# Attention: where the second norm's root stands on GpSimd and its normalisation on VectorE

## Chip, cores and metric

The kernel runs on one core of a Trainium2 chip. The metric is the device time of one execution in microseconds (us), as the median of several runs.

## What is computed

A "macaron" block over 32 sequences of 256 tokens of width 128, in float32: `x += 0.5*ffn(ln(x))`, then `x += attention(ln(x))`, then `x += 0.5*ffn(ln(x))`. The feed-forward is a mixture of 8 experts: each token goes to the expert of its largest affinity, and only the tokens of the highest ranks within the sequence are kept. Attention is causal, with 16 heads of width 8. Cut to what matters here:

```python
def _layernorm(x, axis=-1, eps=1e-05):
    m = jnp.mean(x, axis=axis, keepdims=True)
    v = jnp.var(x, axis=axis, keepdims=True)
    return (x - m) / jnp.sqrt(v + eps)

# attention, on ln(x)
q, k, v = (split_heads(q), split_heads(k), split_heads(v))
att = jnp.einsum('bhqd,bhkd->bhqk', q, k) * scale
att = jnp.where(causal[None, None] == 0, big_neg, att)
att = jax.nn.softmax(att, axis=-1)
x = jnp.einsum('bhqk,bhkd->bhqd', att, v)
# routing of the feed-forward that follows, on ln of the new x
num = jnp.einsum('bsd,ed->bse', inputs, waff)
x_norm = jnp.linalg.norm(inputs, axis=-1, keepdims=True)
aff = num / (x_norm * w_norm[None, None, :] + 1e-09)
ranks = jnp.argsort(jnp.argsort(-aff, axis=1), axis=1)
```

## The kernel before

The program has five stages, each behind a barrier: token statistics, routing, experts, attention with the routing of the second feed-forward, experts again. The change touches attention alone (some 275 to 860 us of the profile).

Attention is a software pipeline written out by hand. `run` (L1207) calls `turn(b, k, has)` on every engine for b from -4 to 35. A turn has NP = 12 steps, `u` = 0 to 11, and works on several sequences at once; `has(o)` says whether sequence b + o exists. Every engine executes its own list in program order, and semaphores join the lists. What a turn does, by sequence:

- b + 4 and b + 3: gather `xa` (GpSimd, steps 2 and 3, L1283), first norm, Q and K in bfloat16 parts (ScalarE L1371, VectorE L1697, L1711), V.
- b + 2 and b + 1: scores by query for the row maxima. TensorE writes one tile `pp` in each step (`scores_by_query`, L1430 to L1437; `QUERY_TILES`, L1121, names which), VectorE reduces it to maxima (L1678). There are two `pp` buffers: a tile waits until the maxima of the tile two before it are done. In steps 0 to 4 these are tiles 7 to 11 of sequence b + 1, in steps 5 to 11 tiles 0 to 6 of b + 2. The maxima go through GpSimd (L1328 to L1334, step 5), TensorE (L1552), ScalarE (L1398) and a transfer on SP's queue (L1231) into `qs` (TensorE's next step 0 waits for that, L1444).
- b: scores by key into `pm` (L1448, L1452), exponential on ScalarE (L1360), causal mask on GpSimd (L1276: `affine_select` on the tile `pt`, one in each step), products with V on TensorE (`times_v`, L1469; tile group 0 in step 6, group 1 in step 9, groups 2 and 3 in steps 0 and 3 of the next turn).
- b - 1: output projection, sum `x2` (VectorE L1727, step 9), `bn_stats` (step 10), mean and variance and then `vare2` (L1592, step 11; it increments `var2`).
- b - 2: the second norm. GpSimd in step 0 raises `vare2` to the powers -0.5 and 0.5 (L1288, increments `rstd2`) and multiplies out `size` (L1290). VectorE in step 2 normalises `x2` to `xn2`, two instructions (helper line L1651, called at L1692). TensorE transposes them in step 3 (L1484, behind `times_v`), ScalarE copies the result out (L1366), TensorE multiplies with the router's weights in step 7 (L1493), VectorE forms affinities in step 8 (L1611).
- b - 3 and b - 4: ranking. VectorE L1623, L1626, L1637, L1641 and `beats` L1687 in steps 0 and 1; GpSimd scatters rows in steps 7 and 9 (L1322).

On VectorE a step runs `route_a`, `place_a`, the maxima of the step's tile, `route_b`, `place_b`, and then the further work. On GpSimd a step begins with the mask. On TensorE a step runs the `pp` tile, the `pm` tile, `times_v` where due, and then `small(u)`, where L1484 is.

Of the kernel before, what the change touches and what calls it, by code (L numbers as in the profile page):

```python
# [14 lines left out]
ALU = mybir.AluOpType  # L15
# [4 lines left out]
D = 128  # L20
# [3 lines left out]
TPB = S // P  # L24
# [14 lines left out]
NQ = 4  # L39
# [10 lines left out]
class Mem:  # L50
# [17 lines left out]
    def sb(self, name, shape, dt=F32):  # L68
        return self.ctx.enter_context(self.nc.sbuf_tensor(name, shape, dt))
# [1031 lines left out]
def attention(nc, m, io, c, x_dram):  # L1101
# [9 lines left out]
    with ctx:  # L1111
# [13 lines left out]
        xa, xr, x2 = two("xa", [P, TPB, D + 2]), two("xr", [P, TPB, D]), [sb(f"x2{k}", [P, TPB, XW]) for k in range(NQ)]  # L1125
        bn, vare = two("bn", [P, TPB, 6]), two("vare", [P, TPB])
        bn2, vare2 = two("bn2", [P, TPB, 6]), two("vare2", [P, TPB, 2])
        xn, xt = two("xn", [P, TPB, D]), two("xt", [P, S])
        xn2, x2t = two("xn2", [P, TPB, D]), two("x2t", [P, S])
# [7 lines left out]
        powers, mhalf = sb("powers", [P, TPB, 2]), sb("mhalf", [P, TPB])  # L1137
# [55 lines left out]
        def wait(eng, s, n, most=None):  # L1193

            n = n if most is None else min(n, most)
            if n > 0:
                eng.wait_ge(s, n)
# [62 lines left out]
        def _(pool):  # L1260
            g = nc.gpsimd
# [6 lines left out]

            def turn(b, k, has):
                for u in range(NP):  # L1270
                    if has(0):

                        wait(pool, exped, b * NP + (u + 1))
                        n = 4 if u % 3 == 2 else 2
                        tile = pt[u % RING][:, :].rearrange("p (h q) -> p h q", h=n)[:, :, 0:P]
                        g.affine_select(out=tile, in_=tile, compare_op=ALU.is_ge, fill=0.0, base=0,  # L1276
                                        pattern=[[0, n], [1, P]], channel_multiplier=-1).then_inc(masked, 1)
                    if u in (2, 3) and has(4):
                        n, j = b + 4, u - 2
# [4 lines left out]
                                                bass.IndirectOffsetOnAxis(ap=c.place[:, n * TPB + j:n * TPB + j + 1], axis=0)).then_inc(xa_in[k % 2], 16)  # L1284
                    if u == 0 and has(-2):
                        n, q = b - 2, k % 2
                        wait(pool, var2, n + 1)
                        g.tensor_tensor(x2[(k - 2) % NQ][:, :, D + 1:D + 3], vare2[q][:, :, :], powers[:, :, :], ALU.pow).then_inc(rstd2, 1)  # L1288
                        wait(pool, rstd2, n + 1)
                        g.tensor_tensor(size[q][:, :], x2[(k - 2) % NQ][:, :, D + 1], x2[(k - 2) % NQ][:, :, D + 2], ALU.mult).then_inc(size_done, 1)  # L1290
                    if u == 1 and has(-2):
# [11 lines left out]
                    if u == 3 and has(-3):  # L1303
                        n, q = b - 3, (k - 3) % 2
# [7 lines left out]
                    if u == 10 and has(-3):  # L1312
                        q = (k - 3) % 2
                        wait(pool, spot_got, b - 2)
                        g.tensor_copy(to[(k - 3) % NQ][:, :], spot_of[q][:, :]).then_inc(to_done, 1)
                    if u in (7, 9) and has(-4):
                        n, j = b - 4, (u - 7) // 2
# [6 lines left out]
                    if u == 5 and has(1):  # L1324
                        n, q = b + 1, (k + 1) % 2
# [9 lines left out]
                    if u == 8 and has(4):  # L1335
                        wait(pool, var1, b + 5)
                        g.tensor_tensor(xa[k % 2][:, :, D + 1], vare[k % 2][:, :], mhalf[:, :], ALU.pow).then_inc(rstd1, 1)

            run(turn)

        @blk.scalar
# [237 lines left out]
        def _(dve):  # L1579
# [39 lines left out]
            def place_a(n, q, u):  # L1619

                if u == 0:
                    wait(dve, aff_done, n + 1)
                    v.tensor_reduce(amax[n % NQ][:, :], aff[:, :, :], axis=AX.X, op=ALU.max).then_inc(amax_done, 1)  # L1623
                if u == 1:
                    wait(dve, weighed, TPB * n + TPB)
                    v.tensor_reduce(wmax[:, :], weight[:, :, :], axis=AX.X, op=ALU.max).then_inc(wmax_done, 1)  # L1626
                if u == 8:
                    wait(dve, turned_out, n + 1)
                    v.tensor_tensor(spot[:, :, :], mr[:, S:S + TPB * E].rearrange("p (j e) -> p j e", e=E),
                                    c.hots[q][:, 0:3 * TPB:3, :], ALU.mult).then_inc(own_spot, 1)  # L1630
# [18 lines left out]
            def normalise(out, x, done):  # L1649
                for j in range(TPB):  # L1650
                    v.scalar_tensor_tensor(out[:, j, :], x[:, j, 0:D], x[:, j, D:D + 1],  # L1651
                                           x[:, j, D + 1:D + 2].to_broadcast([P, D]), ALU.subtract, ALU.mult).then_inc(done, 1)
# [8 lines left out]
            def turn(b, k, has):  # L1661
                for u in range(NP):
                    if has(-2):
                        route_a(b - 2, k % 2, u)
                    if has(-3):
                        place_a(b - 3, (k - 3) % 2, u)
                    for o, w in QUERY_TILES[u]:
                        if has(o):
                            n, q = b + o, (k + o) % 2
                            wait(dve, pre_done, n * NP + (w + 1))  # L1670
                            if w == 0:
                                wait(dve, mp_done, n - 1)
                            if w < 4:
                                out = mx[q][:, 0, :, 2 * w:2 * w + 2].rearrange("p r g -> p g r")
                                src = pp[w % 2].rearrange("p (g r q) -> p g r q", g=2, r=2)
                            else:
                                out, src = mx[q][:, 1, :, w - 4], pp[w % 2].rearrange("p (r q) -> p r q", r=2)
                            v.tensor_reduce(out, src, axis=AX.X, op=ALU.max).then_inc(maxed, 1)  # L1678
# [4 lines left out]
                    if u in (0, 1) and has(-4):  # L1683
                        n, j = b - 4, u
# [1 line left out]
                        wait(dve, ranked, n * TPB + j)  # L1686
                        v.scalar_tensor_tensor(beats[j][:, :], mr[:, j * S:(j + 1) * S], amax[k][:, j:j + 1], c.tie[:, j, :],  # L1687
                                               ALU.subtract, ALU.is_gt, accum_out=x2[k][:, j, RANK:RANK + 1]).then_inc(ranked, 1)
                    if u == 2 and has(-2):
                        wait(dve, rstd2, b - 1)  # L1690
                        wait(dve, x2t_tr, (b - 3) * TPB)
                        normalise(xn2[k % 2], x2[(k - 2) % NQ], xn2_done)  # L1692
                    if u == 3 and has(3):
                        h = (k + 1) % 2
                        wait(dve, a_done, b + 4)
# [3 lines left out]
                    if u == 5 and has(-1):  # L1699
                        q = (k - 1) % 2  # L1700
# [7 lines left out]
                    if u == 5 and has(3):  # L1708
                        q = (k + 1) % 2
# [12 lines left out]
                    if u == 9 and has(-1):  # L1722
                        q = (k - 1) % 2
# [8 lines left out]
                    if u == 11 and has(-1):  # L1732
                        q = (k - 1) % 2
                        wait(dve, rstd2, b - 2)
                        statistics(b - 1, x2[(k - 1) % NQ], bn2[q], vare2[q], bnd2, mv2, var2, True)

            run(turn)
            s = Steps(dve, settled)
            dve.wait_ge(summed, B)
# [76 lines left out]
```

## Time and profile before

| | us |
|---|---|
| median of 3 runs | 1015.39 |
| range of the runs | 1014.93 to 1016.19 |
| the profiled execution | 1012.83 |
| its span | 1011.1 |
| mean granted clock of TensorE | 0.955 |

Busy over the whole span: TensorE 87% (weight loads 66%), VectorE 74%, ScalarE 59%, GpSimd 68%. Stretches differ: attention keeps TensorE and VectorE above 90%, the stages around it do not. So the shares of the whole span say little for one stage; the rows below are read from attention. Durations are of one execution. An instruction shown as x2 is two, one behind the other, with the time from the start of the first to the end of the second; because the engine pipelines, the next one can start before the shown end. In brackets behind a row stands how long the engine sat idle before it, and what ended that.

### The profile page before, as it was taken

The numbers are of one execution on the slowest core, as the hardware profiler recorded it, in microseconds if no ns is written. First come the engines' busy times: TensorE is split into PE (matmuls) and PEld (weight loads), VectorE is DVE, ScalarE is ACT, GpSimd is POOL, SyncE is SP. The second block draws the span as 40 slices with busy tenths as digits, with TensorE's granted clock in tenths as the row PEclk, the third lists the DMA queues.
The fourth block names the chain that finished last, engine by engine and source line by source line (L and its number), as shares of the span: only waits on it lengthen the run. The fifth ranks groups of instructions, "written<-read, shape, count | busy, mean of one in ns | idle before, by whom it ended". The sixth has DMA issues, their size and how long they took to land. (4 is left out here: it accounts for less than half of the span.)

```text
span 1011.1 us, 26251 instructions
## 1 busy us (share of the span) xinstructions
PE 876.8 (87%) x8024; PEld 664.9 (66%) x8057; DVE 748.7 (74%) x2500; ACT 599.8 (59%) x1575; POOL 691.8 (68%) x1245
## 2 busy tenths in 40 slices
PE   5936599999557999999999999999999974899995
PEld 5833499999524566565656566666666542899995
DVE  8879756555247789998998989898989854655552
ACT  2537466666314666666766666666666661666662
POOL 7709578753123678888888888888887774266664
PEclk9999889999858999999999999999999995899998
DMA  7450032222145553545464445455444301222220
GB/s 213 129 186 0 9 74 68 73 70 63 43 93 111 108 107 93 125 95 120 93 118 96 117 99 110 105 106 108 102 109 95 72 18 49 65 74 67 68 65 22
DMA packets 127017, 89.50 MB, mean 89 GB/s; under 512 B 14187, under 2 KB 117536, under 8 KB 126880
## 3 DMA queue, kind: packets, MB, share of 16 engines
q1 hardware_dynamic: 102752, 52.55, 22.9%
q10 hardware_dynamic: 15488, 17.74, 7.8%
q0 software_dynamic: 8640, 17.53, 6.7%
q8 instruction: 68, 1.11, 0.5%
q14 instruction: 69, 0.57, 0.2%
HBM read 52.09 MB, written 35.34 MB: 86 GB/s over the span
## 5 line engine op out<-in xcount | busy, mean ns | idle before, releaser
L1360 ACT ACTIVATE at_pt<-at_pm 128x512 f32<-128x512 f32 x384 | 228.0, 598 | 118.2 <-PE at_pm L1448 89.9
L1678 DVE TENSOR_REDUCE at_mx<-at_pp 128x2 f32<-128x512 f32 (+1 forms) x384 | 259.7, 679 | 43.0 <-PE at_pp L1437 35.7
L1276 POOL TENSOR_SCALAR_AFFINE_SELECT at_pt<-at_pt 128x256 f32<-128x256 f32 (+1 forms) x384 | 188.0, 493 | 57.1 <-ACT at_pt L1360 54.3
L936 ACT ACTIVATE e_ht<-e_ps_h,b1t 128x128 f32<-128x128 f32 x568 | 161.7, 370 | 84.2 <-PE e_ps_h L981 84.1
L981 PE MATMUL e_ps_h<-e_xnt,e_w1own 128*128 128x128 f32 x1136 | 153.3, 280 | 2.0 <-ACT e_xnt L930 1.3
L992 PE MATMUL e_ps_y<-w,e_ht 128*128 x1136 | 149.1, 275 | 0.0
L981 PEld LDWEIGHTS e_ps_h<-e_xnt,e_w1own 128*128 128x128 f32 x1136 | 141.0, 196 | 3.2 <-ACT e_xnt L930 2.0
L992 PEld LDWEIGHTS e_ps_y<-w,e_ht 128*128 128x128 f32 x1136 | 137.8, 192 | 0.0
L900 POOL DMA_INDIRECT out_dram<-e_y,e_x x71 | 82.3, 1159 | 68.1 <-DVE e_y L1062 51.9
L1062 DVE SCALAR_TENSOR_TENSOR e_y<-e_ps_y,e_x 128x256 f32<-128x256 f32 x72 | 30.3, 421 | 110.3 <-PE e_ps_y L992 110.3
L1469 PE MATMUL at_po<-at_pt,vp 128*32 128x256 f32 (+1 forms) x2048 | 109.8, 332 | 1.6 <-POOL at_pt L1276 1.6
L1435 PE MATMUL at_pp<-kb,qs 96*128 96x512 bf16 x256 | 100.1, 391 | 7.4 <-DVE at_mx L1678 6.2
L1448 PE MATMUL at_pm<-qs,kb 128*128 128x256 bf16 x512 | 97.7, 272 | 9.7 <-DMA qs<-at_mt 8.2
L867 POOL DMA_INDIRECT e_x<-rows,gidx x69 | 68.7, 995 | 38.8 <-DVE e_y L1062 21.3
L1469 PEld LDWEIGHTS at_po<-at_pt,vp 128*32 128x32 f32 x2048 | 53.4, 109 | 50.5 <-issue 21.0
L1448 PEld LDWEIGHTS at_pm<-qs,kb 128*128 128x128 bf16 x512 | 47.9, 97 | 48.1 <-DMA qs<-at_mt 15.5
L1322 POOL DMA_INDIRECT buckets<-at_x,at_to x64 | 65.4, 1022 | 20.0 <-issue 19.2
L1054 DVE COPY e_w1own<-w 128x512 f32 x142 | 64.7, 458 | 14.6 <-issue 9.3
L1283 POOL DMA_INDIRECT at_xa<-x,place x64 | 65.9, 1029 | 11.7 <-issue 11.3
L1437 PE MATMUL at_pp<-mask,identb 128*128 128x256 bf16 x256 | 70.9, 277 | 0.0
L1430 PE MATMUL at_pp<-kb,qs 96*128 96x256 bf16 x256 | 50.5, 279 | 7.6 <-DMA kb<-at_qkd 7.1
L1452 PE MATMUL at_pm<-qs,kb 128*128 128x128 bf16 x512 | 49.2, 218 | 2.8 <-ACT at_pt L1360 1.1
(324 smaller groups left out, 1744.5 us busy)
## 6 DMA issues: line engine op xcount, KB each, us to landing
at_qkd<-at_part SPq DMA_DIRECT2D x64, 192.0 KB, 3.0
kb<-at_qkd SPq DMA_DIRECT2D x64, 96.0 KB
qs<-at_qkd ACTq DMA_DIRECT2D x64, 96.0 KB
e_x<-buckets SPq DMA_DIRECT2D x71, 66.0 KB, 1.9
x<-e_y SPq DMA_DIRECT2D x35, 128.0 KB, 1.8
rows<-ts_x ACTq DMA_DIRECT2D x16, 264.0 KB, 3.0
ts_x<-in_x_dram SPq DMA_DIRECT2D x16, 256.0 KB, 3.3
x_by_token<-at_xa SPq DMA_DIRECT2D x32, 128.0 KB
```

Of the source, the lines that this page charges most:

```text
L867: pool.indirect_dma_start(x_row[s][:, j % 2, :], None, rows, bass.IndirectOffsetOnAxis(ap=c.gidx[:, j:j + 1], axis=0)).then_inc(x_in[s], 16)
L900: pool.indirect_dma_start(y_dram, bass.IndirectOffsetOnAxis(ap=to, axis=0), y_row[s][:, j % 2, :], None, bounds_check=T - 1, oob_is_err=Fa ...
L936: last = a.activation(hid_t[j % NB][:, f, :], ps_h[j % NB][:, f, :], ACT.Gelu, bias=c.b1t[:, ds(e, 1), f])
L981: last = te.matmul(ps_h[j % NB][:, f, :], w1_own[j % NB][:, f * P:(f + 1) * P], xn_t[(j // 2) % NX][:, j % 2, :], start=True, stop=True, s ...
L992: last = te.matmul(out, hid_t[j % NB][:, f, :], c.w2[:, ds(e, 1), f, :].rearrange("p a d -> p (a d)"), start=(f == 0), stop=(f == FC - 1))
L1276: g.affine_select(out=tile, in_=tile, compare_op=ALU.is_ge, fill=0.0, base=0, pattern=[[0, n], [1, P]], channel_multiplier=-1).then_inc(ma ...
L1360: a.activation(pt[u % RING][:, :], pm[u % 2], ACT.Exp, scale=SCALE).then_inc(exped, 1)
L1435: te.matmul(out, qs[s][0:ROWS, v - 4, P:S], kb[s][0:ROWS, v - 4, :, :].rearrange("p r q -> p (r q)"), start=True, stop=False, skip_group_c ...
L1437: te.matmul(out.rearrange("p (r q) -> p r q", r=2)[:, :, P:S], c.identb[:, :], c.mask[:, 0:2, :], start=False, stop=True, skip_group_check ...
L1448: last = te.matmul(out[:, i * S:(i + 1) * S], kb[s][:, g + 2 * w + i, r, 0:P], qs[s][:, g + 2 * w + i, :], start=True, stop=True)
L1469: last = te.matmul(out[32 * j:32 * j + 32, (half + 1) * S - cols:(half + 1) * S], values[:, w // 2, at:at + 32], src[:, i * cols:(i + 1) * ...
L1678: v.tensor_reduce(out, src, axis=AX.X, op=ALU.max).then_inc(maxed, 1)
```

## The change

Two blocks move; no instruction is added, removed or reshaped. On GpSimd the wait on `var2` and the power L1288 go ahead of the mask of step 0; the wait on `rstd2` and `size` stay behind it. On VectorE the normalisation of step 2, with its waits, goes ahead of the maxima of step 2.

```diff
             def turn(b, k, has):
                 for u in range(NP):
+                    if u == 0 and has(-2):
+                        wait(pool, var2, b - 1)
+                        g.tensor_tensor(x2[(k - 2) % NQ][:, :, D + 1:D + 3], vare2[k % 2][:, :, :], powers[:, :, :], ALU.pow).then_inc(rstd2, 1)
                     if has(0):
 
                         wait(pool, exped, b * NP + (u + 1))
...
                     if u == 0 and has(-2):
                         n, q = b - 2, k % 2
-                        wait(pool, var2, n + 1)
-                        g.tensor_tensor(x2[(k - 2) % NQ][:, :, D + 1:D + 3], vare2[q][:, :, :], powers[:, :, :], ALU.pow).then_inc(rstd2, 1)
                         wait(pool, rstd2, n + 1)
                         g.tensor_tensor(size[q][:, :], x2[(k - 2) % NQ][:, :, D + 1], x2[(k - 2) % NQ][:, :, D + 2], ALU.mult).then_inc(size_done, 1)
...
                     if has(-3):
                         place_a(b - 3, (k - 3) % 2, u)
+                    if u == 2 and has(-2):
+                        wait(dve, rstd2, b - 1)
+                        wait(dve, x2t_tr, (b - 3) * TPB)
+                        normalise(xn2[k % 2], x2[(k - 2) % NQ], xn2_done)
                     for o, w in QUERY_TILES[u]:
...
-                    if u == 2 and has(-2):
-                        wait(dve, rstd2, b - 1)
-                        wait(dve, x2t_tr, (b - 3) * TPB)
-                        normalise(xn2[k % 2], x2[(k - 2) % NQ], xn2_done)
```

## Rows read from the trace of the kernel before

**Rows 1.** Stretch: us; busy PE, PEld, DVE, ACT, POOL; granted clock; DMA share; GB/s.
```profile
500.00:600.00 100.00, 95.26 (x975) 60.84 (x983) 91.13 (x278) 66.26 (x145) 85.74 (x186) 1.00 0.50 107
```

**Rows 2.** Waits from 365 to 807 us: us in total, times, longest us.
```profile
PEld at_pp L1435 <- DVE at_mx L1678: 19.1, 58, 0.7
...
PEld at_pm L1448 <- DMA qs<-at_mt: 12.4, 12, 1.4
PEld at_mi L1484 <- DVE at_xn L1651: 11.8, 25, 0.7
```

**Rows 3.** VectorE in order of time, one turn: start, us, instruction.
```profile
509.04 0.24 DVE L1592 TENSOR_TENSOR at_vare<-at_x,eps 128x4 f32<-128x4 f32 x1
...
509.88 0.60 DVE L1637 SCALAR_TENSOR_TENSOR at_weight<-at_aff,at_amax,down 128x8 f32<-128x8 f32 x2
510.40 0.47 DVE L1687 SCALAR_TENSOR_TENSOR at_beats<-at_mr,at_amax,tie 128x256 f32<-128x256 f32 x1
...
511.48 0.20 DVE L1641 TENSOR_TENSOR hots<-at_weight,at_wmax 128x48 bf16<-128x48 f32 x1
...
512.00 0.68 DVE L1678 TENSOR_REDUCE at_mx<-at_pp 128x2 f32<-128x512 f32 x1
512.61 0.82 DVE L1651 SCALAR_TENSOR_TENSOR at_xn<-at_x 128x128 f32<-128x128 f32 x2
513.35 0.68 DVE L1678 TENSOR_REDUCE at_mx<-at_pp 128x2 f32<-128x512 f32 x1
```

**Rows 4.** TensorE's weight loads and matmuls in the same turn.
```profile
512.27 0.59 PEld L1469 LDWEIGHTS at_po<-at_pt,vp 128*32 128x32 f32 x16 [0.21 <-POOL at_pt L1276]
513.48 0.20 PEld L1484 LDWEIGHTS at_mi<-ident,at_xn 128*128 128x128 f32 x2 [0.62 <-DVE at_xn L1651]
...
513.76 0.38 PE L1435 MATMUL at_pp<-kb,qs 96*128 96x512 bf16 x1
```

**Rows 5.** The weight loads of L1484 in four other turns.
```profile
381.75 0.20 PEld L1484 LDWEIGHTS at_mi<-ident,at_xn 128*128 128x128 f32 x2 [0.54 <-DVE at_xn L1651]
398.25 0.20 PEld L1484 LDWEIGHTS at_mi<-ident,at_xn 128*128 128x128 f32 x2 [0.46 <-DVE at_xn L1651]
414.36 0.20 PEld L1484 LDWEIGHTS at_mi<-ident,at_xn 128*128 128x128 f32 x2 [0.21 <-DVE at_xn L1651]
...
821.98 0.20 PEld L1484 LDWEIGHTS at_mi<-ident,at_xn 128*128 128x128 f32 x2 [0.41 <-DVE at_xn L1651]
```

**Rows 6.** GpSimd in the turn of rows 3, and ScalarE's exponentials for steps 1 and 2.
```profile
509.24 0.21 POOL L1299 TENSOR_TENSOR aff_sum<-aff_sum,at_aff 128x16 f32<-128x16 f32 x1
510.06 0.41 POOL L1276 TENSOR_SCALAR_AFFINE_SELECT at_pt<-at_pt 128x256 f32<-128x256 f32 x1 [0.61 <-ACT at_pt L1360]
510.44 1.05 POOL L1288 TENSOR_TENSOR at_x<-at_vare,at_powers 128x4 f32<-128x4 f32 x1
...
511.71 0.41 POOL L1276 TENSOR_SCALAR_AFFINE_SELECT at_pt<-at_pt 128x256 f32<-128x256 f32 x1
...
512.38 0.64 POOL L1276 TENSOR_SCALAR_AFFINE_SELECT at_pt<-at_pt 128x512 f32<-128x512 f32 x1
...
510.15 1.23 ACT L1360 ACTIVATE at_pt<-at_pm 128x512 f32<-128x512 f32 x2
```

**Rows 7.** The same instructions of VectorE beside other work of GpSimd, three other turns.
```profile
526.46 0.35 DVE L1637 SCALAR_TENSOR_TENSOR at_weight<-at_aff,at_amax,down 128x8 f32<-128x8 f32 x2
527.82 0.19 DVE L1641 TENSOR_TENSOR hots<-at_weight,at_wmax 128x48 bf16<-128x48 f32 x1
527.68 1.04 POOL L1288 TENSOR_TENSOR at_x<-at_vare,at_powers 128x4 f32<-128x4 f32 x1
...
379.73 0.37 DVE L1641 TENSOR_TENSOR hots<-at_weight,at_wmax 128x48 bf16<-128x48 f32 x1
379.63 0.41 POOL L1276 TENSOR_SCALAR_AFFINE_SELECT at_pt<-at_pt 128x256 f32<-128x256 f32 x1
...
413.71 0.60 DVE L1651 SCALAR_TENSOR_TENSOR at_xn<-at_x 128x128 f32<-128x128 f32 x2
```

## Prediction

> **What bounds the kernel now.** I read the stretches first. Between 500 and 600 us, in the middle of attention, TensorE is busy 95 of 100 us, VectorE 91, GpSimd 86 and ScalarE 66, at a full granted clock [rows 1]. Nothing there has room, so the second view is the waits of that stage [rows 2]. TensorE's weight loads show three real ones: for the maxima of VectorE before a new `pp` tile may be written (19.1 us, 58 times), for the transfer that brings the maxima into `qs` (12.4 us, 12 times), and for the second norm, L1484 behind L1651 (11.8 us, 25 times). The third is what this change can touch. The third view is one turn of each engine in order of time.
>
> VectorE in that turn runs without a gap from `vare2` at 509.04 to the tile 10 maxima at 513.35 [rows 3]. Its last two pieces are the tile 9 maxima (starting 512.00) and the two normalising instructions (starting 512.61); the maxima after them start at 513.35. So the pair costs 513.35 - 512.61 = 0.74 us and the maxima 0.61. TensorE's weight loads go through the products with V at 512.27 and then sit 0.62 us until L1484 may start at 513.48 [rows 4]. A gap of 0.21 stands there also when VectorE is in time (the turn at 414.36 [rows 5]), so the real stall is about 0.41. The next `pp` tile, 11, follows at 513.76, that is 0.28 after L1484. That tile needs the tile 9 maxima, done at 512.68, long before.
>
> **How often.** Stalls at L1484 in 365 to 807 us: 11.8 - 25 x 0.20 = 6.8 us [rows 2]. Two more lie in the drain (one of 0.30, and 0.41 - 0.20 = 0.21 at 821.98 [rows 5]), so 7.3 us. Taken turn by turn from 381.75 (0.54 shown) to 821.98 (0.41 shown) [rows 5], 16 turns stall by 0.28 or more beyond the 0.20, seven by 0.01 to 0.26 (0.93 together), and the others not at all. Later turns, with larger waits, have neither a mask nor maxima in the places that the change swaps.
>
> **Part one, the order on VectorE.** Nothing is added or removed; the pair goes ahead of the tile 9 maxima. The pair would be done some 0.6 us sooner, and L1484 starts when TensorE gets to it, at 513.48 - 0.41 = 513.07. But the sum of the two pieces on VectorE is the same, and tile 11 now waits for the later one: the maxima end where the pair ended, about 513.43, and tile 11 starts about 0.05 behind, at 513.48 in place of 513.76. So the stall doesn't vanish. It changes its place to L1435 of step 4, and what is won is that the two transposes (0.28 us) now run inside it. Per turn that is the smaller of 0.28 and the stall: 16 x 0.28 + 0.93 = 5.4 us. Where TensorE itself came last (414.36 [rows 5]) the maxima, ending where the pair ended, are still in time: nothing is won or lost.
>
> Is it kept? The turn closes on itself: from tile 11 on TensorE works through steps 4 to 10 without waiting for VectorE; VectorE then waits for a new tile, and runs gapless to the pair. All hangs on tile 11, ScalarE's copy L1366 behind L1484 comes earlier, and the transfer of the maxima is issued behind TensorE's step 8, which moves along. I take it as kept.
>
> **Part two, the root on GpSimd.** L1288 lasts 1.05 us and now stands behind the mask of step 0, which waited 0.61 us for ScalarE's exponential [rows 6]. Afterwards it needs only `vare2` (509.04 + 0.24 [rows 3]) and the end of L1299 (509.24 + 0.21 [rows 6]): it runs 509.45 to 510.50. The mask of step 0 then runs at 510.50 and not at 510.06, 0.44 later. Behind it are queued `size`, the mask of step 1, the token copy, L1302, the mask of step 2 and the two gathers of `xa`; all of these but the mask come earlier, the mask of step 1 at about 511.10 and not 511.71, because the idle 0.61 is used (its exponential is done by about 510.8, a half of the pair at 510.15 [rows 6]). The tile of that mask is read by TensorE only in step 6, microseconds later: that hides the 0.44, and it would cost up to 0.44 a turn without this cover. The new wait on `var2` stands ahead of the mask; `vare2` is written before the exponential of step 0 is ready in this turn, so nobody waits. The root itself was done at 511.49 and the pair now wants it at about 511.8, so the earlier root is cover rather than gain (margin 1.3 us in place of 0.3).
>
> **What the moved root does to VectorE's own times.** This is the unknown term. Instructions of VectorE with two inputs in SBUF stretch beside GpSimd's mask. L1637 shows 0.60 us for its pair beside the mask [rows 3, 6] and 0.35 with GpSimd idle [rows 7]. L1641 shows 0.20 clear of the masks [rows 3] and 0.19 beside the root (527.82 [rows 7]), but 0.37 beside a mask (379.73 [rows 7]). The pair L1651 shows 0.82 beside the mask of step 2 [rows 3, 6] and 0.60 where that mask comes later (413.71 [rows 7]). Afterwards the root, not the mask, lies beside L1637: 0.25 saved. The mask of step 1 slides to 511.10 and over L1641: 0.17 lost. The pair still meets the mask of step 2: 0 to 0.15 lost (the latter by the stretch of L1641, the nearest row), or 0.22 gained if it slips by. So the sequence changes by between -0.47 and +0.07. I take -0.05, near the two terms whose neighbours I can place. It pays where the stall is deeper than 0.28, up to the stall: 16 x 0.05 = 0.8 us; its ends are 16 x 0.13 = 2.1 us won by the stall's depth, and 23 x 0.10 = 2.3 us lost.
>
> **Sum.** 5.4 + 0.8 = 6.2 us. The profiled execution took 1012.83 us (span 1011.1, 1.7 around it), so its like would take 1006.6. It lies 2.6 below the median of the runs, 1015.39; the same difference gives 1009.2.
>
> **Rivals.**
> *The sequence clears.* If L1637 and the pair both slip past the masks, VectorE is 0.47 shorter and L1484's whole stall goes, with part of the waits for maxima ahead of it. The turn that ends with the pair at 413.71, 0.60 long [rows 7], lasted 414.36 - 398.25 = 16.11 us, against 16.50 of the one before it (398.25 - 381.75) [rows 5], 0.39 less. 27 turns of that: 10.5 us, 1004.9. Against it: the mask of step 2 comes earlier along with the pair.
>
> *The transfer swallows it.* Twelve turns wait for the maxima to land in `qs` [rows 2]. If landing is set by what else is queued on SP and ScalarE and not by TensorE's step 8, the gain ahead of each comes back as a longer wait. Nine of the gains lie ahead of such a turn: 6.2 - 9 x 0.33 = 3.2 us, 1012.2; if the other turns fall into the same wait, 1015.
>
> *The root holds the port (slower).* Once L1288 lies beside L1637 it could block it until its end, 510.50: then L1637 ends at 510.77 in place of 510.40, 0.37 later, and if the mask gets in between, 0.40 more. Less 0.28, that is 0.09 to 0.49 a turn, over 27 turns 2.4 to 13 us: 1017.8 at the near end. It decides from the point where VectorE's sequence grows by more than 0.28. Against it: L1641 began with two inputs in SBUF while the root ran (527.68 to 528.72) and showed 0.19, as without it [rows 7].
> The Trainium skill, "SBUF — State Buffer", Who interferes with whom, would have it so: a VectorE instruction with two SBUF inputs contends with a GpSimd instruction that reads SBUF, and the loser blocks fully. By that rule, the rows on the masks agree and the row on the root does not.
>
> **How the numbers follow.** Forecast 0.60, at 1009.2, its own range 1006.5 to 1012. Clearing 0.10, swallowed or given back by stretched instructions 0.20, port held 0.10. A difference of 0.2% (2 us) is about the least that a measurement of this kernel can tell from none. Swallowed splits mostly into "same", a little into faster: faster 0.72, same 0.18, slower 0.10. Low end 1004.5, which takes in the clearing; high end 1014.5, which takes in most of the swallowed case and leaves out the port.
>
> **What would show it.** Right: L1484 shows the bare 0.20 in nearly all turns, and L1435 of step 4 a new wait of 0.1 to 0.4 on the maxima; L1637 at 0.35 for its pair; the wait on `qs` no longer than before; the period of a turn about 16.3. Wrong: L1637 at 0.9 or more beside L1288 (port held); the wait for `qs` grown by what L1484 lost (swallowed); or the products with V waiting for GpSimd's mask, if its 0.44 isn't covered. Most fragile is the -0.05 of VectorE's own times.

## The result, and the profile after

| | before | after |
|---|---|---|
| median, us (20 runs each) | 1015.38 | 1013.04 |
| range, us | 1013.09 to 1017.54 | 1009.08 to 1014.77 |
| the profiled execution, its span | 1012.83, 1011.1 | 1013.47, 1011.7 |
| mean granted clock of TensorE | 0.955 | 0.929 |

The ratio is 0.9976, with a 95% interval of 0.9968 to 0.9985: 2.4 us faster (1.5 to 3.2), where 6.2 were forecast. The two profiled executions don't show that difference as it is: before's lay 2.6 us under its median and after's 0.4 over. So below, the traces are compared in stretches of attention, not by their spans.

The stretch and the waits of TensorE's weight loads from 365 to 807 us, in the kernel after. L1683 is L1678 of before, L1449 is L1448, L1485 is L1484 and L1652 is L1651. These rows answer to [rows 1, 2].

```profile
500.00:600.00 100.00, 94.88 (x987) 61.46 (x990) 89.45 (x279) 67.25 (x146) 86.13 (x183) 1.00 0.49 106
```
```profile
PEld at_pm L1449 <- DMA qs<-at_mt: 20.8, 18, 1.7
...
PEld at_pp L1436 <- DVE at_mx L1683: 13.2, 50, 0.8
```

The wait of L1484 on the normalisation, 25 times and 11.8 us before, has fallen to 5 times and 1.0 us. The waits for maxima fell from 19.1 to 13.2 us. But the waits for the transfer that brings the maxima into `qs` grew from 12 times and 12.4 us to 18 times and 20.8 us. TensorE is no busier than before in the middle of attention (94.88 against 95.26).

The same turn as in [rows 3, 4, 6], in order of time: VectorE, then TensorE, then GpSimd.

```profile
508.96 0.20 DVE L1593 TENSOR_TENSOR at_vare<-at_x,eps 128x4 f32<-128x4 f32 x1
...
509.76 0.35 DVE L1638 SCALAR_TENSOR_TENSOR at_weight<-at_aff,at_amax,down 128x8 f32<-128x8 f32 x2
...
511.11 0.19 DVE L1642 TENSOR_TENSOR hots<-at_weight,at_wmax 128x48 bf16<-128x48 f32 x1
...
511.63 0.60 DVE L1652 SCALAR_TENSOR_TENSOR at_xn<-at_x 128x128 f32<-128x128 f32 x2
...
512.16 1.27 DVE L1683 TENSOR_REDUCE at_mx<-at_pp 128x2 f32<-128x512 f32 x2
```
```profile
513.31 0.20 PEld L1485 LDWEIGHTS at_mi<-ident,at_xn 128*128 128x128 f32 x2 [0.20 <-issue]
...
513.59 0.38 PE L1436 MATMUL at_pp<-kb,qs 96*128 96x512 bf16 x1
```
```profile
509.23 1.04 POOL L1273 TENSOR_TENSOR at_x<-at_vare,at_powers 128x4 f32<-128x4 f32 x1
...
510.26 0.40 POOL L1279 TENSOR_SCALAR_AFFINE_SELECT at_pt<-at_pt 128x256 f32<-128x256 f32 x1
...
510.64 0.18 POOL L1291 TENSOR_TENSOR at_size<-at_x 128x2 f32<-128x2 f32 x1
511.28 0.41 POOL L1279 TENSOR_SCALAR_AFFINE_SELECT at_pt<-at_pt 128x256 f32<-128x256 f32 x1 [0.46 <-ACT at_pt L1361]
```

In this turn nearly everything local came as the prediction had it. L1485 shows the bare 0.20; L1638 runs in 0.35 inside the root's 1.04 (in before 0.60, beside the mask); the pair ends ahead of the maxima. Only the mask of step 1 came later than forecast, at 511.28 and not at 511.10. The stall at L1484 is gone in nearly every turn, and yet most of the gain is not in the time.

### The profile page after: what moved, and what is told of

It is laid out like the page before. It is cut to its first block and busy times, and to the rows that moved or that the text cites. A ratio compares the mean times of both kernels' runs of the same rounds, so it can differ in the third digit from the quotient of the medians.

```text
span 1011.7 us, 26251 instructions
## 1 busy us (share of the span) xinstructions
PE 876.1 (87%) x8024; PEld 665.6 (66%) x8057; DVE 742.7 (73%) x2500; ACT 600.6 (59%) x1575; POOL 694.1 (69%) x1245
## 5 line engine op out<-in xcount | busy, mean ns | idle before, releaser
L1683 DVE TENSOR_REDUCE at_mx<-at_pp 128x2 f32<-128x512 f32 (+1 forms) x384 | 258.5, 681 | 48.3 <-PE at_pp L1438 39.8
L1449 PE MATMUL at_pm<-qs,kb 128*128 128x256 bf16 x512 | 98.0, 273 | 16.7 <-DMA qs<-at_mt 15.2
L1449 PEld LDWEIGHTS at_pm<-qs,kb 128*128 128x128 bf16 x512 | 47.3, 97 | 56.7 <-DMA qs<-at_mt 24.7
L1323 POOL DMA_INDIRECT buckets<-at_x,at_to x64 | 65.4, 1021 | 20.7 <-issue 19.9
L1286 POOL DMA_INDIRECT at_xa<-x,place x64 | 65.0, 1015 | 11.9 <-issue 11.5
```

Of the source, the lines that this page charges most:

```text
L1449: last = te.matmul(out[:, i * S:(i + 1) * S], kb[s][:, g + 2 * w + i, r, 0:P], qs[s][:, g + 2 * w + i, :], start=True, stop=True)
```

## The experiments

The expectations speak of theories by letters. D, which stands at the end, is: the root's new place shortens VectorE's sequence, so ScalarE's loads into `qs` start earlier and make the maxima's transfer, issued just ahead of them on SP's queue, land some 1 us late. C had the gathers of `xa`, which come earlier on GpSimd, as the transfers in its way.

What the traces and runs of all kernels showed, in one table. "Waits" are those of TensorE's weight loads for the maxima's transfer, 365 to 807 us. "24 turns" is the time from the L1484 that stands at 381.75 us in before [rows 5] to the one 24 turns later, "last 5" from there to the one five turns later, where the masks end.

| kernel | ratio to before, 95% interval | waits: times, us | 24 turns, us | last 5, us |
|---|---|---|---|---|
| before | 1 | 12, 12.4 | 396.3 | 64.8 |
| before_again | one run | 13, 14.7 | 396.4 | 65.1 |
| after | 0.9976 (0.9968 to 0.9985) | 18, 20.8 | 393.5 | 67.1 |
| both_again | one run | 18, 20.3 | 395.5 | 66.8 |
| norm_only | 0.9945 (0.9928 to 0.9962) | 6, 7.0 | 391.8 | 65.6 |
| norm_again | 0.9928 (0.9910 to 0.9947) | 7, 6.6 | 388.4 | 65.1 |
| norm_third | 0.9944 (0.9923 to 0.9965) | 5, 5.8 | 392.9 | 64.8 |
| root_only | 0.9989 (0.9976 to 1.0003) | 18, 20.8 | 395.6 | 66.8 |
| both_drain_old | 0.9968 (0.9953 to 0.9984) | 21, 22.0 | 392.1 | 66.1 |
| after_mt_act | 1.0090 (1.0070 to 1.0110) | 2, 1.3 | 397.8 | 68.2 |
| norm_early_gather | 0.9936 (0.9914 to 0.9958) | 6, 4.8 | 391.6 | 65.0 |
| both_late_gather | 0.9960 (0.9947 to 0.9973) | 7, 7.1 | 393.3 | 66.5 |
| before_late_gather | 1.0025 (1.0011 to 1.0040) | 3, 3.3 | 399.8 | 65.1 |
| both_loads_wait | 1.0056 (1.0038 to 1.0074) | 2, 2.4 | 399.4 | 69.1 |
| norm_loads_wait | 1.0048 (1.0028 to 1.0069) | 0 | 402.3 | 66.5 |
| drain_loads_wait | 1.0038 (1.0015 to 1.0060) | 1, 1.2 | 401.7 | 66.7 |
| before_loads_wait | 1.0067 (1.0042 to 1.0092) | 0 | 402.2 | 65.9 |
| both_short_hold | 0.9942 (0.9921 to 0.9963) | 2, 2.6 | 391.2 | 68.1 |
| norm_short_hold | 0.9958 (0.9943 to 0.9973) | 3, 2.3 | 391.1 | 65.8 |
| drain_short_hold | 0.9941 (0.9921 to 0.9960) | 2, 2.2 | 388.9 | 65.4 |

**Each half alone.** norm_only has VectorE's half, root_only GpSimd's.

```diff
 norm_only, against before (root_only is the other half of the change)
+                    if u == 2 and has(-2):
+                        wait(dve, rstd2, b - 1)
+                        wait(dve, x2t_tr, (b - 3) * TPB)
+                        normalise(xn2[k % 2], x2[(k - 2) % NQ], xn2_done)
                     for o, w in QUERY_TILES[u]:
...
-                    if u == 2 and has(-2):
-                        wait(dve, rstd2, b - 1)
-                        wait(dve, x2t_tr, (b - 3) * TPB)
-                        normalise(xn2[k % 2], x2[(k - 2) % NQ], xn2_done)
```

> Only VectorE's half: the normalisation ahead of the maxima, the root where it was, behind the mask of step 0. Theory A (the order on VectorE carries the gain, the early root costs in the drain because GpSimd's masks then follow one another without a gap and hold the pair L1651 off: 2.36 us for 0.80 in the changed kernel's trace): this keeps most of the gain and loses nothing in the drain, 3 to 5 us below the kernel before, and the pair of sequence 29 shows under 1 us. Theory B (what L1484 lost is given back in the wait for the maxima's transfer, whatever the root does): 1 to 3 us below, as the changed kernel. If the early root carried the gain: no difference.

> Only GpSimd's half: the root ahead of the mask of step 0, VectorE as before. Theory A: L1637 shows 0.35 for its pair and VectorE's sequence gets 0.1 to 0.25 shorter in most turns, so up to 3 us won in the steady turns, and 2.7 us lost in the drain as in the changed kernel: within 1.5 us of the kernel before. Rival: the root is the half that brings the gain, 2 us or more below.

> VectorE's half alone once more, for a second execution in the trace and more times. Theory C (an early root moves GpSimd's gathers ahead, and with them the landing of the maxima's transfer gets later): L1448's waits for the transfer between 365 and 807 us stay low, under 10 us against 20.8 with the early root; time 4.5 to 6 us below the kernel before. Rival (the waits scatter from one execution to the next, whatever the kernel): they may as well be 15 to 20 us this time.

VectorE's half alone gains more than both: ratios 0.9945, 0.9928 and 0.9944 in three groups of runs, which of 1015.4 us are 5.6, 7.3 and 5.7 us. All three intervals lie below that of the whole change. The root alone gains 1.1 us, with no change inside its interval. In norm_only the waits for the transfer fell, to 6 times; in root_only they rose, to 18, as many as with both halves. So the root on GpSimd brings them. The halves don't simply add: beside the early root VectorE's half is worth only 0.9989 - 0.9976, 1.3 us. There L1484 had less to win, 17 waits of 5.7 us in root_only against 25 of 11.8 us in before.

```profile
PEld at_pp L1435 <- DVE at_mx L1682: 23.0, 66, 0.8
...
PEld at_pm L1448 <- DMA qs<-at_mt: 7.0, 6, 1.5
```

These are the waits of norm_only in the same view. With fewer waits for the transfer there are more for maxima (23.0 against 13.2 us): VectorE catches up while TensorE waits for a transfer, so 1 us of such waits costs less than 1 us of time.

**The last turn with masks.** both_drain_old has both halves, but the root stays behind the mask once there are no more maxima. after_mt_act issues the maxima's transfer from ScalarE's queue.

```diff
 both_drain_old, against after (GpSimd)
-                    if u == 0 and has(-2):
+                    if u == 0 and has(-2) and has(1):
...
                         n, q = b - 2, k % 2
+                        if not has(1):
+                            wait(pool, var2, n + 1)
+                            g.tensor_tensor(x2[(k - 2) % NQ][:, :, D + 1:D + 3], vare2[q][:, :, :], powers[:, :, :], ALU.pow).then_inc(rstd2, 1)
```
```diff
 after_mt_act, against after: four lines of SP go to ScalarE, step 8, behind the copy into mt
-                    wait(sp, mt_out, b + 2)
-                    sp.dma_start(qs[q][ROWS:ROWS + 6, :, :], mt[q % 2][:, :].unsqueeze(1)).then_inc(m_in[q], 16)
+                        wait(act, mt_out, b + 2)
+                        act.dma_start(qs[q][ROWS:ROWS + 6, :, :], mt[q % 2][:, :].unsqueeze(1)).then_inc(m_in[q], 16)
```

> Both halves, but the root goes behind the mask again in the turns that have no maxima left in steps 0 to 4 (the last sequences). Theory A: the pair L1651 no longer takes 2.36 us at the last turn with masks, TensorE's clock stays up there, and some 2.7 us more are won than with the change, 5 us below the kernel before. Rival (the drain's loss was chance, or comes from somewhere else): as the changed kernel, 2.3 us below.

> The changed kernel with the transfer of the maxima issued from ScalarE's queue right behind the copy L1398, not from SP's behind the write of qkd. Theory B (the transfer swallowed the gain, and its landing hangs on what stands ahead of it in SP's queue): the waits of L1448 for the transfer, 20.8 us in 365 to 807 us of the changed kernel, fall by half or more, and the time by 4 to 8 us against the changed kernel, if ScalarE's 0.8 us for the issue costs nothing. Rival (landing is set by the shared DMA engines, not by the queue): waits as before, and the time the same or longer by what ScalarE loses.

The pair of VectorE in the last turn with masks, first in after and then in before; behind them GpSimd beside it, in the same order:

```profile
818.47 2.36 DVE L1652 SCALAR_TENSOR_TENSOR at_xn<-at_x 128x128 f32<-128x128 f32 x2 [2.40 <-POOL at_x L1273]
```
```profile
821.12 0.80 DVE L1651 SCALAR_TENSOR_TENSOR at_xn<-at_x 128x128 f32<-128x128 f32 x2 [2.75 <-POOL at_x L1288]
```
```profile
818.42 0.41 POOL L1279 TENSOR_SCALAR_AFFINE_SELECT at_pt<-at_pt 128x256 f32<-128x256 f32 x1
818.80 0.18 POOL L1291 TENSOR_TENSOR at_size<-at_x 128x2 f32<-128x2 f32 x1
818.94 0.40 POOL L1279 TENSOR_SCALAR_AFFINE_SELECT at_pt<-at_pt 128x256 f32<-128x256 f32 x1
819.30 0.24 POOL L1293 COPY at_x<-token 128x2 int32<-128x2 int32 x1
819.51 0.20 POOL L1303 TENSOR_TENSOR at_pieces<-at_rest_a,at_pieces 128x16 bf16<-128x16 f32 x1
819.68 0.98 POOL L1279 TENSOR_SCALAR_AFFINE_SELECT at_pt<-at_pt 128x512 f32<-128x512 f32 x2
...
820.64 0.24 POOL L1310 TENSOR_TENSOR hots<-hots 128x8 bf16<-128x8 bf16 x1
```
```profile
820.04 1.05 POOL L1288 TENSOR_TENSOR at_x<-at_vare,at_powers 128x4 f32<-128x4 f32 x1
...
821.17 0.19 POOL L1290 TENSOR_TENSOR at_size<-at_x 128x2 f32<-128x2 f32 x1
821.31 0.47 POOL L1276 TENSOR_SCALAR_AFFINE_SELECT at_pt<-at_pt 128x256 f32<-128x256 f32 x1
```

In both the pair waits for the root. In before it begins at 821.12, 0.05 us ahead of `size`. In after the mask of step 0 stands right behind the root and begins at 818.42, 0.05 us ahead of the pair. GpSimd runs without a gap to the end of the masks, and the pair needs 2.36 us in place of 0.80. It is the same with the root early in root_only (2.38), both_again (2.36), both_late_gather and both_loads_wait (2.37 each) and both_short_hold (2.42), and 0.80 in before_again, norm_only, norm_again, norm_third, both_drain_old and drain_short_hold. The start alone doesn't settle it: in after_mt_act the mask also began 0.05 us ahead (831.59 and 831.64) and the pair took only 1.15 us; why is open. The weight load behind the pair then waits, in after:

```profile
820.89 0.20 PEld L1485 LDWEIGHTS at_mi<-ident,at_xn 128*128 128x128 f32 x2 [1.63 <-DVE at_xn L1652]
```

In before it waited 0.41 [rows 5]. The last five turns take 66.8 to 68.1 us in the four profiles with the early root there and nothing else moved but the short hold (after, both_again, root_only, both_short_hold), and 64.8 to 66.1 in before, norm_only, both_drain_old, drain_short_hold and their repeats. The other rows of the table part less cleanly: 66.5 in both_late_gather with the early root, 66.7 in drain_loads_wait without it. TensorE's granted clock between 820 and 830 us, before (first fence) and after (second):

```profile
820.00:825.00 5.00, 3.91 (x52) 2.28 (x53) 1.72 (x7) 3.75 (x8) 4.37 (x12) 1.00 0.00 0
825.00:830.00 5.00, 4.75 (x70) 3.17 (x66) 3.15 (x16) 3.69 (x10) 3.32 (x7) 1.00 0.07 18
```
```profile
820.00:825.00 5.00, 3.63 (x34) 2.20 (x38) 2.13 (x6) 2.76 (x6) 2.40 (x7) 0.81 0.00 0
825.00:830.00 5.00, 4.75 (x58) 3.19 (x54) 2.16 (x13) 2.70 (x8) 2.88 (x6) 0.85 0.05 17
```

Part of these windows of after thus ran at 1.2 GHz, behind the gap of 1.63 us; all of before's ran at 2.4. In root_only, with the same gap, it stayed at 1.00, so the lower clock may follow and need not. In time, both_drain_old gains 0.8 us on after (0.9968 against 0.9976), inside both intervals: seen in the traces, not settled by the times.

after_mt_act took nearly all waits for the transfer away, but its copy into `mt` ended later behind L1484 than the 7.76 us of an undisturbed turn: by 10.3 us in sum over the 24 turns, by 1.4 in after. I put that down to ScalarE being busy with its own issues. By the ratios it was 11.6 us slower than after (0.0114 of 1015.4), and shows only that this queue is no place for the transfer.

**The gathers.** Three kernels move the two gathers of `xa`, one to steps 1 and 2, two to step 3.

```diff
 norm_early_gather, against norm_only
-                    if u in (2, 3) and has(4):
-                        n, j = b + 4, u - 2
+                    if u in (1, 2) and has(4):
+                        n, j = b + 4, u - 1
```
```diff
 both_late_gather, against after (before_late_gather, against before, is the same)
-                    if u in (2, 3) and has(4):
+                    if u == 3 and has(4):
...
+                        for j in range(TPB):
```

> VectorE's half alone with the gathers of xa in steps 1 and 2 in place of 2 and 3, about 1 us earlier. Theory C: the waits of L1448 for the transfer rise from 7.0 us to 15 or more, and the time by 2 to 4 us above VectorE's half alone. Rival: waits and time as VectorE's half alone, or lower.

> The changed kernel with both gathers of xa in GpSimd's step 3, behind its mask, in place of steps 2 and 3: some 1.5 us later for the first and 1 us for the second. Theory C: L1448's waits fall from 20.8 us to under 12 and the time to that of VectorE's half alone plus the drain's loss, about 1011. Rival (the gathers have nothing to do with it): waits 15 to 22 us, time 1013; if the gathered rows come late for bn_stats in step 6, VectorE shows waits for xa there and the time rises.

> The kernel before with both gathers in step 3. Theory C: its 12.4 us of waits for the transfer shrink, but L1484 still waits for VectorE, so the time falls by 2 us at most. Rival: no difference in the waits.

Theory C falls: with early gathers norm_early_gather has 6 waits, as norm_only, and its ratio is the same. Late gathers do take waits away, 18 to 7 and 12 to 3, but not for nothing: before_late_gather is slower than before. That `xa` reaches the first norm later, and with it all that follows down to ScalarE's loads, would explain both. It fits the order of issues below: the loads start less than 0.6 us behind the transfer in 5 of 24 turns of both_late_gather, against 21 of after. The price of it I didn't follow turn by turn.

**The order of issues.** Set side by side, the turns that wait and those that don't differ in when ScalarE's first loads (L1354, step 9) start behind SP's transfer (L1231). Two turns of after, one behind the other. Turn one, with the wait that follows it:

```profile
517.91 1.32 SPq L1226 DMA_DIRECT2D at_qkd<-at_part  x2
521.10 0.81 SPq L1231 DMA_DIRECT2D qs<-at_mt  x1
```
```profile
521.59 0.87 ACTq L1354 DMA_DIRECT2D qs<-at_qkd  x2
```
```profile
525.13 0.11 PEld L1449 LDWEIGHTS at_pm<-qs,kb 128*128 128x128 bf16 x2 [1.39 <-DMA qs<-at_mt]
```

Turn two, in which nothing waits for the transfer:

```profile
537.75 0.81 SPq L1231 DMA_DIRECT2D qs<-at_mt  x1
```
```profile
538.48 0.87 ACTq L1354 DMA_DIRECT2D qs<-at_qkd  x2
```

521.59 - 521.10 = 0.49 us in the one, 0.73 in the other. Over the 24 turns of the twelve kernels down to before_late_gather in the table, without after_mt_act: loads less than 0.6 us behind the transfer, 168 turns, 125 of them with a wait, 1.09 us on average; 0.6 us or more, 120 turns, 4 with a wait. Among the 168, if the issue of the first two loads took under 0.85 us, 109 of 109 waited; if it took longer, 16 of 59. One number takes in both conditions: when the issue of these two loads ends, counted from the start of the transfer's issue (521.59 + 0.87 - 521.10 = 1.36 us in turn one, 1.60 in turn two). Where it ended by 1.43 us, 124 of 124 turns waited; where it ended at 1.45 or later, 5 of 164. By kernel, near starts are 20 of 24 in before, 21 in after and in root_only, but 7 in norm_only. Within before's 20 the 12 that waited are just those whose issue ended by 1.43; why it was stretched in the others is open.

The loads wait for `qkd` to land. L1226 was issued 4.93 us behind L1484 on average in norm_only, 4.65 in after and 4.62 in before. I take this for what the root does: from `vare2` to the pair VectorE takes 2.73 us in after and 2.87 in norm_only (averages of 24 turns), L1637 being shorter, and the writes to `qkd` come 0.28 us earlier. The 0.14 of VectorE is half of that; the other half I can't place. Against before the shift is far smaller: the near starts stay at 20 or 21, and L1226 stands at 4.60 in root_only against before's 4.62. But starts under 0.50 us, of which all 116 waited, go from 11 in before to 18 in root_only, so hundredths of a microsecond decide there. That the root's place brings the waits is shown by the kernels; the path by which it does is argued from averages.

**Holding the loads.** Four kernels let ScalarE's first loads wait for the sum `x2` (VectorE, step 9), which puts them some 1.1 us behind the transfer.

```diff
 both_loads_wait, against after (likewise in norm_loads_wait, drain_loads_wait, before_loads_wait)
                     if u in (9, 10, 11) and has(3):
+                        if u == 9:
+                            wait(act, x2_done, b)
                         q_rows(b + 3, (k + 3) % NQ, (k + 1) % 2, u - 9)
```

> The changed kernel, with ScalarE's first two loads of qs in step 9 (L1354) held until VectorE's sum x2 of that step is done, some 0.5 us later. Theory D (these loads, when they are issued 0.5 us behind the transfer of the maxima, lie on the same DMA engines and make it land 1 us late; in the traces so far all 72 turns with loads at 0.5 us and an issue of 0.7 us waited, and 3 of some 95 with loads at 0.6 us or later): L1449's waits fall from 20.8 us to under 3 and the time by 3 to 5 us against the changed kernel, to 1008 to 1010. Rival (start of the loads is only a sign of something else, of the landing of qkd for one): waits 15 us or more, time as the changed kernel.

> VectorE's half alone, with the same hold on the loads. Theory D: its 6.6 to 7.0 us of waits go too, 1 to 2.5 us below VectorE's half alone, 1006 to 1008. If the whole difference between the halves was the loads: as both halves with the hold, plus the drain's 1 to 2.5 us.

> Both halves, the root behind the mask in the last turns, and the hold on the loads. Theory D and the port in the drain together: 1 to 2.5 us below both halves with the hold. It is the best of all if the early root then pays by itself (L1637 at 0.35).

> The kernel before with the hold. Theory D: the 12.4 us of waits for the transfer go to under 3, but L1484 waits for VectorE in those turns too, so the time falls by 0 to 2 us only; L1484's stalls rise from 11.8 us. Rival: waits as before the hold.

The waits went, as D has it: 18 to 2, 6 to 0, 21 to 1, 12 to 0. The times that I expected of it were wrong: all four are slower than before. The view of the waits of both_loads_wait says where the time went:

```profile
PEld at_pp L1433 <- DMA kb<-at_qkd: 11.4, 18, 1.3
...
PEld at_pm L1451 <- DMA qs<-at_mt: 2.4, 2, 1.5
```

Tile 0 of step 5 now waits for the loads of `kb` and `qs` themselves. They have less slack than the 0.6 us of the hold. So it was shown that the start of the loads makes the transfer late, but not what that costs. Where the two meet, on the DMA engines as theory D has it or elsewhere, no run here shows.

**A shorter hold.** The loads wait for the maxima of the tile of step 9, which puts them at least 0.75 us behind the transfer. Two kernels repeat after and before as they are.

```diff
 both_short_hold, against after (norm_short_hold, against norm_only; drain_short_hold, against both_drain_old)
                     if u in (9, 10, 11) and has(3):
+                        if u == 9:
+                            wait(act, maxed, (b + 2) * NP + 5)
                         q_rows(b + 3, (k + 3) % NQ, (k + 1) % 2, u - 9)
```

> The changed kernel with one wait added on ScalarE: its first loads into qs (L1353, step 9) start only once VectorE has taken the maxima of the tile of step 9, some 0.75 us behind SP's transfer of the maxima in place of 0.5 (the longer hold of the runs before stood at 1.05). Nothing is left out. Theory D (the transfer lands late where the loads start 0.5 us behind it and run unhindered): the 18 waits of L1449 for the transfer go to 4 or fewer; the loads' own landing slips by 0.25 us only, so tile 0 of step 5 waits little for kb (under 0.4 us in a turn, in place of the 1.3 of the long hold); steady turns 392 us or less, median 1009 to 1011.5. Rival (the loads' landing has no slack at all, each 0.1 us of hold is paid in step 5): waits for kb of 0.8 us and more in most turns, median 1013 or above. Rival (the time of the loads has nothing to do with it): 15 waits or more for the transfer, median as the changed kernel's, 1013.

> VectorE's half of the change alone, with the same short hold of ScalarE's first loads. Its six to seven waits for the transfer should go (7.0 us in sum), and only turns whose loads start at 0.5 are moved. Theory D: 2 waits or fewer for the transfer, steady turns 386 to 390 us, median 1006 to 1009.5. Rival (no slack in the loads' landing): waits for kb in step 5, median 1012 or above, as with the long hold (1020.9).

> The changed kernel as it stands, profiled a second time, to see how far the waits for the transfer of the maxima differ between executions. If they are set by the order of issues, as theory D has it: again 15 to 21 waits at L1449, 17 to 23 us, VectorE's pair of the last turn with masks at 2.2 to 2.5 us. If they are chance: 6 to 14 waits.

> The kernel before, profiled a second time: if the order of issues sets the waits, again 10 to 14 of them for the transfer, 11 to 14 us, and the pair of the last turn with masks at 0.8 us. If they are chance, the number may lie as far off as that of the changed kernel, 18.

The waits of both_short_hold, and its issues in the turn shown of after:

```profile
PEld at_pp L1438 <- DVE at_mx L1685: 26.4, 77, 0.8
...
PEld at_pm L1451 <- DMA qs<-at_mt: 2.6, 2, 1.4
...
PEld at_pp L1433 <- DMA kb<-at_qkd: 1.6, 5, 0.4
```
```profile
521.09 0.81 SPq L1231 DMA_DIRECT2D qs<-at_mt  x1
```
```profile
521.85 0.85 ACTq L1354 DMA_DIRECT2D qs<-at_qkd  x2
```

Now the waits are gone and tile 0 waits 1.6 us in all. The ratio is 0.9942 where after has 0.9976: one added wait gives 3.5 us back, and both halves together then reach what VectorE's half has alone. Of the 18.2 us of waits removed, 13.2 came back as waits for maxima (26.4 against 13.2). In norm_short_hold there was little to remove, and it lies at 0.9958, no better than norm_only and not as good as expected. The repeats say that the waits are the kernel's and not an execution's: 18 in both profiles of after, 12 and 13 in those of before.

> Both halves of the change, with both causes of the loss taken away: the short hold of ScalarE's first loads (until VectorE has taken the maxima of the tile of step 9), and the root behind the mask in the turns without maxima, as in the kernel before. If the two causes are separate and are all that the root costs: 3 waits or fewer for the transfer, VectorE's pair of the last turn with masks at 0.80 us, steady turns 391 us as in both_short_hold (391.2), from there to the end 66 us (68.1 there), median 1.5 us below both_short_hold's ratio of 0.9942: 0.992 to 0.994. Rival (the drain's loss is made good elsewhere, as both_drain_old hinted with 0.9968 against 0.9976): ratio 0.994 or above.

> VectorE's half alone a third time, beside the version with both halves and both mends, against the same runs of the kernel before. Its two ratios so far were 0.9945 and 0.9928, so 0.9925 to 0.995; 5 to 8 waits for the transfer. If it stays at or below drain_short_hold, the root's place on GpSimd brings nothing even when its two costs are gone.

drain_short_hold has the shortest 24 turns but one and the pair at 0.80 us, and the last five turns at 65.4 us in place of 68.1. Its ratio, 0.9941, is that of both_short_hold and of norm_third (0.9944). The drain's loss is thus not seen in the times, and its rival (made good elsewhere) can't be excluded: the intervals, 4 us wide, could hide 2 us. The best kernels are VectorE's half alone and this one, some 6 us under before. The half alone is the simpler.

## Why the prediction was wrong

The forecast was 1009.2, with its own range 1006.5 to 1012; it came to 1013.04, inside the wide range (1004.5 to 1014.5), and faster by a little over 0.2%.

*Part one, the order on VectorE.* Right that L1484's stall goes. In after the maxima of tile 9 became what tile 11 waits for: 0.15 to 0.28 us in 10 of 24 turns, where 0.1 to 0.4 was named as the sign. In the three profiles of VectorE's half alone no such wait shows; there the waits for maxima grew in step 2, from 7.9 us in before to 11.1 to 11.5. Alone it gained 5.6, 7.3 and 5.7 us where 5.4 stood in the sum, but that fit is partly luck: the waits for the transfer fell along with it, from 12.4 to between 5.8 and 7.0 us, which the sum didn't have. Where they could not fall, the half is worth less: 1.3 us from root_only to after, with 18 waits and 20.8 us in both, and 1.9 us from before_loads_wait to norm_loads_wait (1.0067 and 1.0048), with none in either, though there the waits for `kb` grew from 5.6 to 14.3 us. In both pairs the intervals overlap. The 5.4 us for the order alone is thus not shown.

*Part two, VectorE's own times.* Right in sign, and near in size. L1637 fell to 0.35 in nearly every turn, and L1641 was not lengthened in the turn shown, since the mask of step 1 still waited 0.46 us for its exponential and came at 511.28, not 511.10. From `vare2` to the pair VectorE took 3.45 us on average in before, of which the maxima that stood between are 0.61, and 2.73 in after: 0.11 less, where the sum had 0.25 - 0.17 = 0.08 for these instructions. The pair slipped by in this turn (0.60 us in place of 0.82); over the 24 turns it averaged 0.76 against 0.80. One end of this term was mis-set: 23 x 0.10 = 2.3 us doesn't follow from a sequence that is 0.07 longer, which gives 1.6.

*The root "is cover rather than gain".* This is the first step that failed. I took its new place to cost nothing as long as the masks were covered, and looked only for who waits for GpSimd. I did not follow what a shorter VectorE sequence lets start earlier. It moved the writes of `qkd`, and with them ScalarE's loads, to within 0.5 us of the maxima's transfer: 21 of 24 turns with near loads in after, 7 in norm_only. In before they were near already, in 20 turns; from there the root tipped the waiting turns from 12 to 18. In the last turn with masks I had named the pair's stall of 0.41 [rows 5] as something to win, and it became 1.63.

*"Is it kept? ... I take it as kept."* This is the second step that failed, and the larger. "The transfer of the maxima is issued behind TensorE's step 8, which moves along" is right of its issue (7.78 us behind L1484 in before and 7.79 in after, in turns without a stall), and wrong of its landing. The waits for it went from 12.4 us to 20.8, where the prediction had "no longer than before". For VectorE's half alone they fell and the time with them; with the root the change kept 2.4 of the 6.2 us.

*The rivals.* "The transfer swallows it" is what happened: its price, 1012.2 to 1015, holds the 1013.04, and its condition, that landing is set by what else is queued on SP and ScalarE, is the one found, though the prediction did not see which half of the change would trigger it. It had 0.20. The trace of before spoke for more: twelve turns already waited for that transfer [rows 2], and the prediction never looked at which turns these were. Set side by side with the issues of ScalarE, before's trace alone would have shown 12 waits in the 20 turns with near loads and none in the other four. "The sequence clears" was half right on VectorE. "The root holds the port" was wrong at its place: L1638 began 0.53 us into the root and took 0.35.

The Trainium skill, "SBUF — State Buffer", Who interferes with whom, says that a VectorE instruction with two SBUF inputs contends with a GpSimd instruction that reads SBUF, that the ports they share are an exclusive lock, and that the order of issue decides who blocks. By that rule, the last turn with masks agrees in who was held: the mask began 0.05 us ahead of the pair and the pair took 2.36 us; in before the pair began (821.12) ahead of `size` and took 0.80. In how long, it does not: the first mask lasted 0.41, and with the same start the pair took 1.15 in after_mt_act. For the root, at 1.04 us, the trace does not agree over its whole length.

*What stays open.* Why the issue of ScalarE's loads is stretched to 0.9 us and more in some turns, in which the transfer then mostly lands in time. How much VectorE's half is worth by its order alone. Why the longer hold costs before 6.8 us, with only 5.6 us of waits for `kb`. And whether the drain's 1 to 3 us in the traces is real time.

## What to carry to other kernels

Ahead of "the rest moves along", list what the shortened engine triggers (here two issues of DMAs) and against what it will then run; a wait that already occurs in a part of the turns is the first to look at, and comparing the turns with and without it gives its condition before anything is changed. Time a two-part change by its halves: here one half alone gained 5.6 to 7.3 us and both together 2.4. Read what else moved before calling a half's gain its own: beside the early root the same half was worth 1.3 us. In a drain, where nothing else fills the gaps, look at the same lines again: an order that is right in the steady turns met GpSimd's gapless run there.

## What the runs showed of the hardware

- A small transfer (48 rows of 256 bfloat16 values) on SP's queue lands in time if the issue of the two loads on ScalarE's queue ends 1.45 us or more behind the start of its own issue (159 of 164 turns without a wait), and keeps TensorE waiting for 1.1 us on average if it ends by 1.43 us (124 of 124, twelve profiles). The Trainium skill, "DMA: Bandwidth & Descriptors", Issuing engines are not separate DMA queues, says that transfers of all issuing engines interleave on the same 16 DMA engines. By that rule, the late landing agrees; why the line lies between 1.43 and 1.45 us, no run here explains.
- VectorE's normalising pair took 2.36 to 2.42 us beside GpSimd's gapless run of masks when a mask began 0.05 us ahead of it (six profiles; 1.15 in a seventh, after_mt_act), and 0.80 when it began first.
- GpSimd's power of 1.04 us, which reads four values in each partition, did not lengthen VectorE's L1638 at all (0.35, as with GpSimd idle [rows 7]).
